# A four-layer transformer kernel on one core: nine batches' rounded x made beside the first mixture, and three smaller moves

## The reference, cut to what matters

```python
x = x + tanh(g_xattn[1]) * L1_xattn(_layernorm(x), ctx, ...)   # the same form for every part
# inside L1_xattn
ln_out = _ln(hidden_states, ln_w, ln_b)                        # a second norm on the normed x
xq = fp8_roundtrip(bf16(clip(ln_out / in_scale, -448, 448)))   # four in_scales: q, k, v, qx
q, k, v, qx = (einsum(xq * in_scale, w) * w_scale for each)
# then two attentions (own keys; keys from ctx), concatenated, rounded again and projected
# L2_xattn: q_nope = (q_c @ W_uq), k_nope = (kv_c @ W_uk), out = attn(v = kv_c @ W_uv) @ W_o
# L2_ffn:   rmsnorm of the normed x, 8-bit rounding, ternary weights
```

## Time and profile before

| what | value |
|---|---|
| median of the three runs | 2374.85 us |
| the profiled execution's own time | 2371.28 us |
| its span, first to last instruction | 2369.5 us |
| mean granted PE clock | 0.960 of full |
| busy: PE, DVE, ACT, POOL | 88%, 79%, 57%, 53% of the span |
| M0, first up-projection to last down-projection | 153.5 to 416.5 us |
| L1's attention, first projection to last output | 445.3 to 1305.0 us |
| M1; L2 attention; L2 feed-forward; L3 | from 1306; 1645; 2015; 2116 us |

### The profile page before, as it was taken

One profiled execution on the slowest core, in us unless ns is written; L12 is line 12 of the kernel. 1 busy time (PEld: TensorE's weight loads), 2 busy tenths in 40 slices (PEclk: granted clock), 3 DMA queues, 4 the chain that ended last, 5 costly groups with the idle time before them and its releaser, 6 DMA issues.

```text
span 2369.5 us, 42812 instructions
## 1 busy us (share of the span) xinstructions
PE 2097.0 (88%) x14151; PEld 1748.7 (74%) x14158; DVE 1874.7 (79%) x3844; ACT 1344.1 (57%) x3389; POOL 1267.1 (53%) x1789
## 2 busy tenths in 40 slices
PE   5969999389999988999998899997899999559997
PEld 2348888278888877888887688886788887236665
DVE  5866665699999988999998677677587886777886
ACT  2223332588888877888885433333344555667783
POOL 4913333489999988898997211110344444741222
PEclk9989999699999999999999899998899999888998
DMA  4201110300000020000000400001000000010001
GB/s 136 82 36 72 72 72 1 129 14 17 14 19 15 21 85 15 19 17 15 21 6 1 130 21 26 22 21 54 12 8 8 8 6 1 1 50 19 24 24 37
DMA packets 38634, 79.99 MB, mean 34 GB/s; under 512 B 5904, under 2 KB 25680, under 8 KB 34480
## 3 DMA queue, kind: packets, MB, share of 16 engines
q1 hardware_dynamic: 38416, 77.24, 9.8%
HBM read 64.65 MB, written 12.58 MB: 33 GB/s over the span
## 4 chain that ended last, share of the span: by engine, by line
PE 58%; POOL 15%; DVE 14%; issue 7%; ACT 5%; DMA 0%; DVEq 0%; SPq 0%; ACTq 0%; POOLq 0%
PE bank L505 7%; PE bank L869 6%; PE bank L1360 4%; PE bank L328 4%; POOL l_tiny L1695 3%; PE bank L885 3%; PE bank L524 3%; PE bank L1375 3%; PE bank L1397 3%; POOL l_cat L1746 3%; PE bank L1384 2%; PE bank L2479 2%; PE bank L1867 2%; PE bank L1366 2%; POOL l_yq L1712 2%
## 5 line engine op out<-in xcount | busy, mean ns | idle before, releaser
L1360 PE MATMUL bank<-l_wr,l_xq 128*128 128x256 f32 (+1 forms) x1024 | 214.3, 352 | 8.0 <-ACT l_raw L1469 8.0
L869 PE MATMUL bank<-m_xr,m_wgr 128*128 128x512 f32 x864 | 211.2, 393 | 1.9 <-DVE m_xr L988 1.9
L869 PEld LDWEIGHTS bank<-m_xr,m_wgr 128*128 128x128 f32 x864 | 158.4, 189 | 32.4 <-issue 2.4
L1695 POOL TENSOR_TENSOR l_tiny<-l_tiny,l_minus_half 128x6 f32<-128x6 f32 x128 | 175.5, 1371 | 10.7
L1360 PEld LDWEIGHTS bank<-l_wr,l_xq 128*128 128x128 f32 x1024 | 159.3, 193 | 25.7 <-issue 8.8
L1397 PE MATMUL bank<-l_wpr,l_cat 128*128 128x256 f32 x1024 | 168.5, 308 | 1.9 <-POOL l_cat L1746 1.9
L1483 ACT ACTIVATE xn_T<-bank,l_head_b,l_head_w 128x512 f32<-128x512 f32 x128 | 99.6, 778 | 119.0 <-PE bank L1408 119.0
L787 POOL TENSOR_TENSOR m_wgr<-m_wg,m_wgr 128x512 fp32r<-128x512 f32 x18 | 23.2, 1291 | 263.4 <-ACT m_wgr L776 263.4
L1627 DVE TENSOR_TENSOR l_raw<-l_raw,l_tiny 128x768 f32<-128x768 f32 x128 | 159.5, 1246 | 0.1
L1375 PE MATMUL bank<-xn_T 128*128 128x128 f32 x1024 | 139.6, 279 | 18.2 <-ACT xn_T L1455 16.6
L1746 POOL TENSOR_TENSOR l_cat<-l_yo,l_eo 128x512 fp32r<-128x512 bf16 x128 | 150.4, 1175 | 4.5 <-DVE l_yo L1571 3.1
(11 more groups left out here) (342 smaller groups left out, 6265.4 us busy)
## 6 DMA issues: line engine op xcount, KB each, us to landing
l_stage<-in_l_w SPq DMA_DIRECT2D x8, 1024.0 KB, 4.8
l_centred<-l_stage SPq DMA_DIRECT2D x6, 1024.0 KB, 4.1
l_stage<-l_centred SPq DMA_DIRECT2D x6, 1024.0 KB, 4.8
m_unsplit<-in_m_w SPq DMA_DIRECT2D x14, 384.0 KB, 3.4
m_wg<-in_m_gu SPq DMA_DIRECT2D x18, 256.0 KB, 2.7
x_norm<-in_ctxT_b SPq DMA_DIRECT2D x32, 128.0 KB, 2.1
l_stage<-in_l_wp SPq DMA_DIRECT2D x4, 1024.0 KB, 4.9
l_saved<-l_xs SPq DMA_DIRECT2D x16, 256.0 KB, 2.0
```

The costliest lines, as they stand in the source:

```text
L869: r = e.matmul(banks[2 * (n % 2) + half][:, :], WGR[:, u % 2, a, k, half, :], XR[:, b, k, cols], start=k == 0 and m == 0, stop=k == KT - 1 ...
L1360: r = e.matmul(to, XQ[:, q % 2, v, k, :], WR[:, j, part, k, h0 * P:h1 * P], start=k == 0 and part == 0, stop=k == KT - 1 and part == 1)
L1695: pool_own.did(e.tensor_tensor(r0, var, minus_half[:, :], ALU.pow))
```

## The change

What it does, part by part:

1. **Nine batches ahead** (`x_ahead`, AHEAD = 9). In M0, batches 0 to 8 are normed with the double norm's root, transposed into the bank `aux`, copied, scaled and rounded, one each in steps 24, 27, 29, 34, 38, 41, 43, 48 and 52 (the transpose's step n; the norm is in n - 1, the copy and scaling on ACT in n to n + 2, rounding on DVE in n + 3 and n + 4), and stored to `l1_saved` by SP between its weight transfers. Their roots come from POOL (`pow`) between the centrings. L1's attention fetches these nine by DMA; batches 9 to 15 are made as before. `moe0`'s rounded x keeps two groups, not four.
2. **L1's start.** The weights' first two pieces stand ahead of the norm, not inside it; the norm's table is no longer loaded early; the engines other than DVE begin at M0's end. The output weights move to steps 13 to 16 (ACT) and 14 to 17 (low parts, on DVE, not POOL); two later weight loads move from steps 12 and 14 to 17 and 18.
3. **One root for double norms**, and no copy of the variance in any norm.
4. **L2's attention**: the absorbed products and ctx's first loads begin at M1's end, ahead of the norm; values and output first; ACT copies them. The norm's transposes go through two banks.

In `moe0` the lines added stand at the ends of step n of PE, of ACT and, behind `weight_means`, of DVE; in `l1_attention` the `fill_out_low` added is DVE's and the one changed POOL's.

```diff
@@ layernorm
-        def newton_rstd(e, var, y, t2, eps, shifted, powered, beside=None):
...
+            eps2 = {"once": None, "twice": LN_EPS, "rms": 1e-6}[kind]
-                dve_own.did(e.tensor_copy(var2, var))
-                first = newton_rstd(e, var, rstd[:, :], t2, LN_EPS, shifted(1), powered(1), beside[0])
...
+                if eps2 is None:
+                    e.tensor_scalar(var, var, LN_EPS, None, ALU.add).then_inc(shifted.sem, 1)
                 else:
-                    first.then_inc(done.sem, 1)
+                    e.tensor_scalar(var, var, 1.0 + eps2, LN_EPS * eps2, ALU.mult, ALU.add).then_inc(shifted.sem, 1)
+                if beside:
+                    beside(e)
+                e.wait_ge(*powered(1))
@@ moe0: tensor, scalar, vector
+            turn_at = {TILES * (g + 1) + t: 4 * g + m for g in range(3) for m, t in enumerate((10, 13, 15, 20))
+                       if 4 * g + m < AHEAD}
...
+                    if n in turn_at:
...
+                        turn_ahead(e, b, aux)
...
+                    if n in turn_at:
+                        put_ahead(e, turn_at[n], aux)
+                    if n - 1 in turn_at:
+                        affine(e, turn_at[n - 1], 0)
+                    if n - 2 in turn_at:
+                        affine(e, turn_at[n - 2], 1)
...
+                    if g >= 1 and t == 6:
+                        spread(e, g - 1)
+                    if g >= 1 and t == 9:
+                        newton(e, g - 1)
+                    if n + 1 in turn_at:
+                        norm_ahead(e, turn_at[n + 1])
+                    if n - 3 in turn_at:
+                        quantise(e, turn_at[n - 3], (0, 1, 2))
+                    if n - 4 in turn_at:
+                        quantise(e, turn_at[n - 4], (3, 4))
+                quantise(e, AHEAD - 1, (3, 4))
                 add_group(e, GROUPS - 1)
...
-            return [bn(B), down(N), hi(N), shareK(GROUPS)]
+            return [bn(B), down(N), hi(N), shareK(GROUPS)] + ahead_stored
@@ first_loads, first_centres
+            ahead_stores = ((), (), (), (), (0,), (1, 2), (3,), (4, 5))
                     e.dma_start(room[:, i % 2, :], A["l1_w"][f]).then_inc(w_in.of(i), 16)
+                    for b in ahead_stores[i]:
+                        store(e, b)
...
                 for i in range(G):
+                    if i == 3:
+                        power(e, 0)
+                    if i == 5:
+                        power(e, 1)
                     centre_weights(e, i)
+                power(e, 2)
@@ l1_attention
-            LOADS = (0, 1, 4, 5, 12, 14, 75, 76, 78, 79)
+            LOADS = (0, 1, 4, 5, 17, 18, 75, 76, 78, 79)
-            out_at = {9: 0, 10: 1, 11: 2, 12: 3, 81: 4, 82: 5, 83: 6, 84: 7}
+            out_at = {13: 0, 14: 1, 15: 2, 16: 3, 81: 4, 82: 5, 83: 6, 84: 7}
...
-            stage(scalar=first_weights)
-            ends = layernorm(ends, "twice", transposed=False, beside=(first_low, second_low))
+            stage(scalar=first_high, vector=first_low)
+            ends = layernorm(ends, "twice", transposed=False, load_root=False)
...
+                begin(e, ahead_stored)
                 for q in range(2):
+                    e.dma_start(XS[:, q, :], saved[q]).then_inc(s_fetch.of(q), 16)
...
+                    if 14 <= s < 18:
+                        fill_out_low(e, s - 14)
-                    if s in out_at:
+                    if s in out_at and out_at[s] >= J:
                         fill_out_low(e, out_at[s])
@@ l2_attention
-            stage(tensor=prepare_tensor, vector=prepare_vector)
-            ends = prepared_ends + [segf(1), put(2)]
+            stage(tensor=absorb_tensor, scalar=absorb_scalar)
+            ends = layernorm(ends, ring=2) + [loaded(n_loaded), put(4), put_q(1), segf(1)]
+            stage(vector=absorb_vector)
```

More of the change, by code:

```diff
@@ L147, in start, with layernorm @@
             return [set_(1), tanh(1), eyeb(1), bn(B)] + [x(1) for x in xload]
-        def newton_rstd(e, var, y, t2, eps, shifted, powered, beside=None):
[L151 to L168, removed]
+        def layernorm(ends, kind="once", transposed=True, counted=True, beside=None, load_root=True, between=None, ring=4):
+            eps2 = {"once": None, "twice": LN_EPS, "rms": 1e-6}[kind]
             bn = signals("x_counted", 0 if counted else B)
-            shifted = signals("var_shifted", 1 + twice)
-            powered = signals("var_powered", 1 + twice)
+            shifted = signals("var_shifted", 1)
+            powered = signals("var_powered", 1)
             done = signals("rstd_done", 1)
@@ L221, in roots @@
                 e.activation(rstd[:, :], var, ACT.Sqrt).then_inc(powered.sem, 1)
[L222 to L228, removed]
+                if between:
+                    between(e)
             def tensor(e):
@@ L417, in moe0_weights, with moe0 @@
             return (load, split, lower), (high, low, router, pick), [w_low(TILES), picked(1)]
-        def moe0(ends, weights, scratch, beside):
+        def moe0(ends, weights, scratch, beside, ahead):
             high, low, router, pick = weights
@@ L800, in moe1 @@
             stage(sync=sync)
-            ends = layernorm(ends, transposed=False, between=(first_high, None))
+            ends = layernorm(ends, transposed=False, between=first_high)
             norm = signals("x_normed", B)
@@ L1425, in turn_x @@
                 r.then_inc(s_xtr.sem, 1)
-            TURNS = tuple(b for b in range(1, B) if b != 2)
             def tensor(e):
-                begin(e, ends)
-                turn_x(e, 0, 0)
+                begin(e, m0_ends)
                 for s in range(END):
@@ L1795, in prepare_tensor, with absorb_scalar @@
                                  start=True, stop=True)
                 r.then_inc(absorbed.sem, 1)
-                for h in range(H):
-                    pair, odd = h // 2, h % 2
-                    r = e.matmul(banks[2 + pair // 2][odd * C:(odd + 1) * C, (pair % 2) * D:(pair % 2 + 1) * D],
-                                 wuvT[:, h, :], wo[:, h, :], start=True, stop=True)
-                r.then_inc(absorbed.sem, 1)
-            def prepare_vector(e):
-                begin(e, prepared_ends)
+            def absorb_scalar(e):
+                begin(e, moe_ends)
+                for n in range(4):
+                    e.wait_ge(*absorbed(n + 1))
+                    e.copy(VO[:, 2 * n:2 * n + 2, :].rearrange("p a d -> p (a d)"), banks[4 + n][:, :]).then_inc(put.sem, 1)
```

390 lines of the change are left out of this document (253 added, 137 removed).

## The result

The changed kernel took 2361.58 us (median of 7 runs, 2357.11 to 2370.65) beside 2380.03 us for the kernel before (7 runs): ratio 0.9932, 95% interval 0.9919 to 0.9945. It is faster, as forecast, but by 16 to 18 us of 2380 and not by 26 of 2371, and the time lies at the slow end of the forecast's range, 13.1 us above the 2348.5. Another set of runs gave 2358.43 (ratio 0.9917, 0.9894 to 0.9941), 19 us. The profiled execution took 2360.09 us (span 2358.3, clock 0.956).

The account below looks back on a forecast made before the run. PE was taken to bound M0 (busy 261 of 265 us), one dependent chain L1's start. 20 + 5.9 + 5.5 + 2.4 + 0.8 - 8.3 = 26.3 off 2371.3 gave 2345.0; with 3.6 to the median, 2348.5 us, range 2336 to 2362.

Parts of the forecast that it names:

- L1's start, 20: From M0's end to item 4 squared in L1: item 4 at 40.2 us against 60.0, gain 20, bounds 12 and 26.
- the three items to item 4 at 6.0: In L1's start, items 2 to 4 were given 6.0 us each, the mean distance of before, covering casts and low parts.
- Fewer x beside items, 5.9: L1's items 10 to 24 go from 6.53 to 6.14 us each: gain 5.9, at least 3, at most 8.
- M0, 8.3: M0 pays 8.3 us for transposes, two waits of PE, rounding and its later end; bounds 2 and 18.
- The two waits: In M0, PE idles for a batch's norm at the ends of steps 24 and 38: 2.4 and 1.4 us.
- The rounding: Batches' rounding on DVE in M0, mostly hidden: 1.3 us charged in steps 29 to 48, 1.1 at the end.
- the transposes were put at 2.1: In M0, PE gains 18 transposes, nine steps with 0.23 us more each: cost 2.1.
- L2's attention, 5.5: Values' products ahead of the norm: first product 4.1 us earlier, 1.4 from the clock; gain 5.5, bounds 2 and 9.
- 8.8 and 0.8 for two banks instead of four: In L2's attention, from root to last copy: 8.8 us for the batches as before, 0.8 more for two banks.
- With work nearer ahead I expect part of it at the higher, 1.4: Behind L2's first product, part of PE's 10.2 us of work runs at the higher clock: gain 1.4.
- One root, 2.4: In L2's "rms" norm, one root instead of two and no copy of the variance: gain 2.4 us.
- The copies' 0.8: The variance's copy dropped in four other norms on the path (L0, M0, M1, L3's last): gain 0.8 us.

## Why the forecast of the gain was too high

*L1's start, 20: right, a little small.* Items 0 and 1 came where the working put them. The step that was cautious is the three items to item 4 at 6.0; they took 5.1 (39.39 less 24.24, by 3). Found 22.5.

*Fewer x beside items, 5.9: right in kind, low.* 7.7 to 8.5. Items 10 to 24 gained 5.7 in the first trace, as forecast; the rest is 1.3 between items 4 and 10, where batches 3 to 5 had been made, and 1.6 from 24 to 28, where batch 8 had been rounded. The bound "at most 8" was passed.

*M0, 8.3: too low; 12.0.* The two waits were forecast at 3.8 and removing them gave 4.7. Their places and lengths were right (2.27 for 2.4, 1.23 for 1.4); the step that failed is that a wait costs its own length. The first cost 3.9, as the granted clock behind it was 0.57 for 4 us; the second cost 0.8. The rounding was forecast at 2.4 and gave 2.3, about half of it in the third wait. A term is missing altogether: 1.6 to 1.9 for the address of a tile, seen in steps in which none of the added instructions run. That leaves 3.1 to 3.4 of the 12.0, where the transposes were put at 2.1; the 1.0 to 1.3 between them isn't explained.

*L2's attention, 5.5: wrong; it lost 1.0.* Two steps failed, the first on the way to the first product, which was to gain 4.1 and gained 1.6. The values' products, put at 5.5 us, took 6.2 behind a wait of 3.84. From the root to the last copy it took 11.2 us, where the working had 8.8 and 0.8 for two banks instead of four. The lower clock was in the 8.8 already (0.56 before, 0.60 now, during the transposes), so the term that was too small is that of the banks. The second step is the clock behind the first product. "With work nearer ahead I expect part of it at the higher, 1.4" is what came in three of the eight traces with this order, which gained about 1.5 there; in the other five, both of the changed kernel among them, it was the reverse and 2.6 were lost. The bound "2" was above the result.

*One root, 2.4: 2.0 where it stands.* The 1.9 lost behind it, in L2's rows of h, is no price of it, since the kernel with both roots and the new order of L2's attention loses as much (76.7); it had no term in the sum. The copies' 0.8 can't be seen apart.

*The base.* The sum was made on one execution of 2371.3, and 3.6 were added for the median of three. Over 73 runs in five sets the medians of before are 2377 to 2380.6, 6 to 9 above that execution: 1.4 to 2.3 of it are M0's first three steps. Beside the changed kernel's first set it was 2380.03, 5.2 above the 2374.85 of the forecast. A forecast of the difference would have been spared this; the time was not.

So, found: -22.5 - 8.1 + 12.0 + 1.0 - 2.0 + 1.9 = -17.7, and 0.8 to 4.3 back behind item 28, so 13 to 17; beside the second trace of before the two of the changed kernel are 14.6 and 16.7 us shorter. That the time still fell inside the range is luck in part: L1's two terms gave 4.7 more than forecast, which hid almost half of the 10.2 by which M0 and L2's attention missed.

## To carry over

Where TensorE sets the pace, give a new wait on its queue a price of its own, with what the products behind it may lose at the lower clock (here 3.9 us for 2.27, and 0.8 for 1.23), and put what it waits for ahead of everything in that step that has slack. Work that was moved into an idle stretch of L2 helped here only once TensorE's gaps were closed too: the order of a root and four copies on another engine was worth 7 us in the medians. When tiles are added to a scratch area, look whether the untouched products still come at their old distance.

## What the runs showed of the hardware

- A wait of TensorE of 2.27 us in a stretch where it was otherwise full was followed by 4 us at a granted clock of 0.57; with the wait gone the clock stayed at 1.00. So it was in all eight traces with the wait and all five without; behind the wait of 1.23 the clock stayed up.
- The same twelve products take 2.80 or 2.76 us by the address of the tile that they read x from, at the same clock. The Trainium skill (SBUF — State Buffer, "Who interferes with whom") says that TensorE never waits on anyone at that memory; the rows show a pace that differs and not what TensorE would wait for, so no run here shows whether that holds.
- 32 transposes, copied out by ACT, took 6.5 us through four banks at a granted clock of 0.56, and through two 9.1 at 0.60 and 7.4 at 1.00.
- The same code gives L2's stretch 146.5 or 151.3 us, and L3's 182 or up to 202; the longer ones are at the lower clock for longer.
